# A graph layer's node pipeline shortened from eight steps to six, with its parameters prepared in two parts

## The reference

```python
h = relu(layernorm(x))                              # no gain, no offset
xn = layernorm(h, g1, b1)
msg = relu(xn[src] + edge_attr)                     # 25,000 edges
aggr = segment_sum(msg, dst, 50000)                 # edges come sorted by dst
u = relu(((1 + eps_gin) * xn + aggr) @ Wg1 + bg1) @ Wg2 + bg2      # the two GIN products
x2 = h + u
xn2 = layernorm(x2, g2, b2)                         # the second norm
f = gelu(xn2 @ Wf1 + bf1) @ Wf2 + bf2               # Wf1 is 128 x 512
return x + x2 + f
```

## Time and profile before

| | us |
|---|---|
| median of 3 runs | 1072.53 (1070.97 to 1072.89) |
| profiled execution, its own time | 1073.02 |
| its span, first to last instruction | 1071.3 |
| PE busy | 992.9 (93%) |
| DVE busy | 978.7 (91%) |
| ACT busy | 844.3 (79%) |
| POOL busy | 799.9 (75%) |

### The profile page before, as it was taken

One profiled execution on the slowest core, in us unless ns is written; L12 is line 12 of the kernel. 1 busy time (PEld: TensorE's weight loads), 2 busy tenths in 40 slices (PEclk: granted clock), 3 DMA queues, 4 the chain that ended last, 5 costly groups with the idle time before them and its releaser, 6 DMA issues. The chain is left out here.

```text
span 1071.3 us, 23085 instructions
## 1 busy us (share of the span) xinstructions
PE 992.9 (93%) x6684; PEld 850.1 (79%) x6684; DVE 978.7 (91%) x3499; ACT 844.3 (79%) x2158; POOL 799.9 (75%) x510
## 2 busy tenths in 40 slices
PE   1336999999999999999999999999999999999998
PEld 1225888888888888888888888888888888878887
DVE  5577999999999999999999999999999999988752
ACT  1247888888888888888888888888888888878773
POOL 6488787787787787887887877888878878866610
PEclk9858999999999999999999999999999999999999
DMA  7566676788887655555555554555565654443311
GB/s 234 139 189 161 161 191 185 177 245 233 234 242 216 134 135 130 135 135 127 138 136 123 138 142 118 139 142 117 142 140 114 143 141 112 120 102 92 58 57 40
DMA packets 110469, 156.87 MB, mean 146 GB/s; under 512 B 24836, under 2 KB 50608, under 8 KB 110335
## 3 DMA queue, kind: packets, MB, share of 16 engines
q1 hardware_dynamic: 70358, 128.99, 37.6%
q0 software_dynamic: 37760, 25.66, 19.3%
q10 hardware_dynamic: 2216, 0.66, 0.3%
HBM read 90.61 MB, written 64.61 MB: 145 GB/s over the span
## 5 line engine op out<-in xcount | busy, mean ns | idle before, releaser
L520 ACT ACTIVATE n_act<-p_f,bf1e_col 128x512 f32<-128x512 f32 x392 | 255.9, 679 | 149.4 <-PE p_f L875 141.5
L447 POOL DMA_INDIRECT aggr_sums<-e_merged,e_index x196 | 322.8, 1647 | 65.8 <-issue 49.8
L917 PE MATMUL p_out<-wf,n_act 128*128 128x128 f32 x3136 | 370.6, 276 | 0.0
L917 PEld LDWEIGHTS p_out<-wf,n_act 128*128 128x128 f32 x3136 | 357.6, 191 | 4.0
L456 POOL TENSOR_TENSOR n_rstd<-n_var,minus_half 128x12 f32<-128x12 f32 (+2 forms) x102 | 256.4, 2514 | 116.4 <-DVE n_var L827 59.6
L436 POOL DMA_INDIRECT e_x<-in_x,e_cols x196 | 214.6, 1095 | 61.6 <-issue 58.9
L875 PE MATMUL p_f<-n_z2T_high,wf_low 128*128 128x512 f32 x392 | 207.0, 528 | 11.9 <-issue 7.0
L875 PE MATMUL p_f<-n_z2T_high,wf_high 128*128 128x512 f32 x392 | 154.6, 395 | 0.0
L875 PE MATMUL p_f<-n_z2T_low,wf_high 128*128 128x512 f32 x392 | 153.9, 393 | 0.0
L672 DVE BATCH_NORM_STATS2 n_stat<-n_x 128x6 f32<-128x256 f32 x392 | 139.6, 415 | 0.1
L532 ACT ACTIVATE p_gout<-n_relu,n_rstd 128x128 f32<-128x128 f32 x392 | 129.3, 367 | 5.4 <-DVE n_x L799 5.2
(11 more groups left out here) (85 smaller groups left out, 1433.5 us busy)
## 6 DMA issues: line engine op xcount, KB each, us to landing
n_x<-in_x SPq DMA_DIRECT2D x97, 256.0 KB
n_aggr<-aggr_sums SPq DMA_DIRECT2D x97, 256.0 KB
out_dram<-n_out SPq DMA_DIRECT2D x97, 256.0 KB
aggr_sums<-zeros SPq DMA_DIRECT2D x26, 512.0 KB, 3.2
e_dst<-in_dst_rows SPq DMA_DIRECT2D x49, 256.0 KB
e_attr<-in_attr SPq DMA_DIRECT2D x48, 256.0 KB
aggr_sums<-zeros SPq DMA_DIRECT2D x12, 1024.0 KB
e_x<-in_x,e_cols POOLq DMA_INDIRECT x196
```

The costliest lines, as they stand in the source:

```text
L447: nc.gpsimd.indirect_dma_start(out=aggr, out_offset=bass.IndirectOffsetOnAxis(ap=e_index[0:r, s, j:j + 1], axis=0), in_=e_merged[0:r, s, j ...
L520: nc.scalar.activation(n_act[:, k, :, 0:b.rows], p_f[k % 2][:, :, 0:b.rows], ACT.Gelu, bias=bf1e_col[:, k:k + 1]).then_inc(s_act, 1)
L917: last = nc.tensor.matmul(p_out[0:b.rows, j, :], n_act[:, k, j, 0:b.rows], wf2[:, k, :], start=False, stop=(k == KF - 1), skip_group_check ...
```

## The change

A block now passes through six stages, node(0) to node(5). The second GIN product is in the step of the first, `node(2)`, together with the transposition of `n_in`; the second norm with its transposition is in `node(3)`; both products of the feed-forward part are in `node(4)`, and `n_out` in `node(5)`. SP stores at `node(7)`. The orders within a step change with it. The parameters that only the later stages need are prepared by DVE at the end of step 1 (`finish_parameters`), and the waits for them move to their first use. SP sets the first part of `aggr` to zero right after its seventh transfer, ahead of the second chunk's loads, and no longer waits for a gather.

```diff
-NODE_LAG = 7
-SP_LAG = 9
+NODE_LAG = 5
+SP_LAG = 7
...
             sp.dma_start(o_dst[:], dst_rows).then_inc(s_order_in, 16)
+            sp.wait_ge(s_zeros, 1)
+            set_to_zero(range(zero_halves_begun(-1)))
             first_chunks(step, *range(1, LEAD - 1))
-            sp.wait_ge(s_zeros, 1)
-            sp.wait_ge(q_gather[1], 16 * J)
-            set_to_zero(range(zero_halves_begun(-1)))
...
-                b, ending = node(1), node(4)
+                b, ending = node(1), node(3)
...
-            act.wait_ge(s_bias, 1)
-            act.wait_ge(s_bf1, 1)
-            branch(act, EDGE_LAG, 6, step)
+            branch(act, EDGE_LAG, 4, step)
...
+            def finish_parameters():
                 dve.wait_ge(s_wf1, 1)
                 dve.wait_ge(s_wf1_mean, 1)
...
             first_chunks(step, *range(LEAD))
+            prepare_parameters()
             half_chunk(step)
-            prepare_parameters()
...
+                if (b := first) is not None and b.is_number(1):
+                    finish_parameters()
...
+            def second_product(b, ks):
+                for k in ks:
+                    pe.wait_ge(s_act, b.at * KF + (k + 1))
+                    for j in range(J):
+                        last = nc.tensor.matmul(p_out[0:b.rows, j, :], n_act[:, k, j, 0:b.rows], wf2[:, k, :],
+                                                start=False, stop=(k == KF - 1), skip_group_check=True)
+                if ks[-1] == KF - 1:
+                    last.then_inc(s_fout, 1)
...
-                if (b := seventh) is not None:
+                if (b := fifth) is not None:
                     pe.wait_ge(s_z2T_low, b.at + 1)
-                    first_product(b, (0, 1))
-                if (b := fourth) is not None:
+                    first_product(b, range(KF))
+                    pe.wait_ge(s_x2b, b.at + 1)
+                    second_product(b, (0, 1))
+                if (b := third) is not None:
+                    pe.wait_ge(s_nin, b.at + 1)
```

More of the change, by code:

```diff
@@ L578, in step @@
                                          ACT.Relu).then_inc(s_emsg, 1)
[L579 to L583, removed]
+                if 0 in halves and 1 in halves:
+                    merged_rows(edge(3))
                 if (b := node(2)) is not None:
@@ L793, in step @@
             def step(node, edge, halves, apart):
[L794 to L795 removed]
+                first, third, fourth = node(0), node(2), node(3)
+                if (b := fourth) is not None:
                     r = b.rows
@@ L911, in step @@
                     last.then_inc(s_tin, 1)
-                if (b := seventh) is not None:
-                    pe.wait_ge(s_x2b, b.at + 1)
-                    for k in range(KF):
-                        pe.wait_ge(s_act, b.at * KF + (k + 1))
-                        for j in range(J):
-                            last = nc.tensor.matmul(p_out[0:b.rows, j, :], n_act[:, k, j, 0:b.rows], wf2[:, k, :],
-                                                    start=False, stop=(k == KF - 1), skip_group_check=True)
-                    last.then_inc(s_fout, 1)
+                if (b := fifth) is not None:
+                    second_product(b, (2,))
+                if (b := third) is not None:
+                    pe.wait_ge(s_inT, b.at + 1)
+                    reached(pe, s_gT, b.at)
+                    if b.is_number(0):
+                        pe.wait_ge(s_bias, 1)
+                    nc.tensor.matmul(p_g[:, :, 0:b.rows], wg1[:], n_inT[:, b.slot(2), :, 0:b.rows],
+                                     start=True, stop=True).then_inc(s_g, 1)
+                if (b := fourth) is not None:
+                    pe.wait_ge(s_z2, b.at + 1)
+                    reached(pe, s_z2T_low, b.at)
+                    for j in range(J):
+                        last = nc.tensor.transpose(p_z2[:, j, 0:b.rows], n_z2[0:b.rows, b.slot(2), j, :],
+                                                   ident[0:b.rows, 0:b.rows])
+                    last.then_inc(s_tz2, 1)
+                if (b := fifth) is not None:
+                    second_product(b, (3,))
+                if (b := third) is not None:
+                    pe.wait_ge(s_gT, b.at + 1)
+                    pe.wait_ge(s_nh, b.at + 1)
+                    for j in range(J):
+                        last = nc.tensor.matmul(p_gout[0:b.rows, j, :], n_gT[:, b.slot(2), j, 0:b.rows], wg2[:],
+                                                start=False, stop=True, skip_group_check=True)
+                    last.then_inc(s_gout, 1)
                 if 0 in halves and (c := edge(3)) is not None:
```

122 lines of the change are left out of this document (55 added, 67 removed).

## The result

| | before | after |
|---|---|---|
| median, us | 1072.71 (4 runs) | 1156.1 (1155.89 to 1156.41, 4 runs) |
| profiled execution, its own time, us | 1073.02 | 1155.89 |
| its span, us | 1071.3 | 1154.1 |
| ratio | | 1.078, 95% interval 1.0763 to 1.0797 |

A forecast was written before the change was run, and what follows sets the result against it. PE and DVE were taken as both full in the middle. To 1073.0 us came 45 pairs at 2.1 us (+94.5), the end (-10.8) and the start (0): 1156.7, median 1156 us, 7.8% slower; range 1120 to 1188.

The forecast's parts named there:

- Group 3 and the gap: PE, first product: group 3 still waits for gelu 1, starting 3.36 us (odd step) and 2.95 (even) after group 0.
- That is 0.86 us for each step: PE, each middle step: p_g, no longer issued between the groups, adds its 0.86 us, 1.72 for a pair.
- n_z2's wait: PE before the transposition of n_z2: waits 0.2 us (odd) and 0.3 (even) for ACT; taken as 0.5 a pair.
- DVE's 0.1: Middle pairs: 0.1 us taken off the sum for what of the 20.00 us was DVE's bound and not PE's.
- The loop through all engines: Middle, hand-overs among the engines: they fit with only 0.1 to 0.3 us to spare; upper end 0.6 us more a pair.
- Rival 3: Middle: the slack is missing and each pair waits for the whole loop, over 2.8 us a pair; 1188 us and more; chance 0.06.
- PE's busy share in the middle: Sign in the changed trace's middle: PE's busy share down to some 90%, with idle time before groups 2 and 3.
- The end: From the first step without a chunk: six steps in place of eight, 57.8 us in place of 68.6, -10.8 us.
- The start: Up to step 6: first chunk some 7 us sooner, but steps 4 and 5 become full; taken as 0, bounds -7 to +5.
- Rival 1: Middle: PE's new idle time is absorbed, DVE's 20.0 us a pair stays the bound; 1055 us; chance 0.11.
- Rival 2: Middle: n_z2 never late and part of p_g finds another gap, about 1.0 us a pair; 1107 us; chance 0.07.
- Rival 4: Whole kernel: the end's gain and a smaller loss of 0.24 us a pair cancel; 1073 us; chance 0.03.

## Why the prediction came out right, and where its account was wrong

**Group 3 and the gap: right.** 3.36 and 2.95 us were forecast, and the trace has these to the hundredth. The kernel before with p_g moved, and n_gT and p_in with it, has a pair 1.75 us longer (1.72 in the sum).

**"That is 0.86 us for each step": right in the kernel before, wrong as a cause in the changed one.** The sum laid p_g's 0.86 and the wait for n_z2 end to end as two causes. They are two roads side by side; the paragraph on n_z2 had both, PE at 8.13 and n_z2 at 8.34, but did not draw from it that 0.86 us less on PE would be worth nothing. The sum is right, and not by luck, because it is just PE's row plus what ACT's row is longer. But p_g alone is worth nothing in the changed kernel (1157.5 with a quarter of it), and n_z2 alone only the 0.38 us a pair by which ACT's road is longer. One description covers both, as I read the rows: the road from gelu 1 over group 3, half of p_out, p_in, n_inT and n_z to p_z now lies within one step, and before, p_z read the n_z2 of the step before.

**n_z2's wait: mechanism right, term a little large.** 0.5 forecast, 0.38 by the shortened n_z2. The rest is that p_z follows p_g after 0.92 us there and not after the 0.86 that the sum took. The forecast places were near: n_inT at 6.57 of the odd step, 6.59 in the trace; n_z done at 8.34, p_z starting on it at 8.41. ACT did wait for p_in (0.37 us), as laid out. With DVE's 0.1 taken off, the two terms gave +2.1 a pair; the trace has 999.8 / 45 = 22.22 against 904.6 / 45 = 20.10, +2.12.

**The loop through all engines: right.** n_x2 comes 0.86 us after PE's step start (0.7 forecast), and in the middle of the kernel PE has no wait for it. POOL's factor for n_z2 is there at 6.6 of the even step and wanted at 6.75 (6.5 and 6.7 forecast). DVE is idle for about 2.2 us of the pair (22.10 - 19.88), 2 forecast. The version with the last quarter moved shows how narrow it is: 0.7 us more and the next first product waits. Rival 3 was the next one in line; the small reordering brought about its first part. One sign was read too boldly: PE's busy share in the middle was forecast at some 90%, and it is 21.03 of 22.10 us, 95%, since the modelled ends of matmuls cover a part of the waits.

**The end: right.** 57.8 us forecast, 57.7 found; steps of 10.1 (1096.38 to 1126.70 is three of 10.1), then 9.78 (9.8), then 7.43 (7.7). In that step the forecast had the last block's whole norm chain as the longer row; the trace has only its end. ACT's n_z2 is done at 1141.78, but PE is at its 24 matmuls of p_out until about 1142.4, and only from there, over p_z, n_z2T_high and n_z2T_low, does PE wait, 0.15 us at 1143.91. The old pipeline's end was 68.6.

**The start: inside its bounds, a little better than taken.** e_merged came at 30.4 (32 forecast), step 4 at 74.30 (73.7) and step 6 at 96.58 (98), -1.6 in place of 0. The version with the old start splits this: its step 6 begins at 103.81, so the full steps 4 and 5 cost 103.81 - 98.16 = 5.65 us, and the new start gives 103.81 - 96.58 = 7.23 us back (7 forecast). At the end of the kernel the new start is worth 6.5 us in the changed kernel and 5.4 in the kernel before. So the sum's "net 0" was a gain of 7.2 and a loss of 5.6 or 5.7. POOL's wait for the first copy fell from 12.71 to 3.78 us.

**Rivals.** Rival 1 needed group 3 at about 2.1 us: it stayed at 2.95 and 3.36. That holds for the rule of the Trainium skill behind it too (Perfetto Trace Analysis, section Optimizing Tensor Performance): it has groups rotate through banks so that the reading of one overlaps the matmuls of the next, and with two banks in rotation a part of the readings stayed visible here, since ACT has other work between two gelus. Where that other work was taken out of the way, the groups did come closer together (3.2 us), and the wait appeared elsewhere. So closing the gap is not enough by itself. Rival 2 (1.0 us a pair) had half the loss and was not near. Rival 4 fell with the pairs.

## What to carry to other kernels

An idle gap on the fullest engine, left by a wait for another engine, can be a place where a matmul is free: in the kernel before, p_g's length cost nothing there, and its being moved out of it, with the orders that went with that, cost 1.75 us of 20. In six stages p_g can't stand in the gap, since it needs the n_inT of its own step; a pipeline of seven, which would let it, was not tried. Bringing dependent stages into one step turns slack of a whole step into a road within it. So before the stages are joined, lay out the road over all engines and compare it with each engine's own row. And when a sum of two terms agrees with the measurement, the terms need not be the causes. Cut each alone and both together: here it was nothing, 17 us, and 70.

## What the runs showed of the chip that I had not expected

**The full clock came sooner where steps 4 and 5 were full.** In the stretch from 80 to 100 us the granted clock is 1.00 in the changed kernel, with PE busy 18.81 us of 20, where the earlier trace rows has 0.75 with PE busy 10.67. The changed kernel with the old start has 0.98 there, with PE busy 18.70 us, so it is not the new start that does it. Nor does the new start bring it in the kernel before, as its stretch shows:

```profile
80.00:100.00 20.00, 11.78 (x47) 8.44 (x47) 17.19 (x67) 14.24 (x37) 16.04 (x11) 0.66 0.53 125
```

There the mean of 0.66 lies between the levels of 1.2 and 2.4 GHz, and its first matmul of the first product takes 0.80 us at 92.63, where the same instruction at 74.30 of the changed kernel takes 0.50 us. That the changed kernel's fuller steps 4 and 5 got a part of their cost back as clock is likely from these rows, but no run separates it.

**Early transfers of zeros delay the first gathers, and it doesn't matter.** With SP's four transfers of zeros ahead of the second chunk's loads, ACT loads its table at 10.56 us (7.05 before) and starts the first e_relu at 15.37 (14.13 before). In the two versions run side by side POOL issues the first gathers at the same times, but DVE, which waits for the first rows, starts on them at 14.82 us with the early zeros and at 12.95 without. The first e_relu is at 15.89 and 14.02, yet the first chunk's e_merged comes at 30.88 and 30.95: the 1.9 us are gone by the third e_relu, since the chunk that it belongs to is waited for less (3.00 against 5.40 us).
